# Attention loops: joining a group's chunk maxima one VectorE instruction later, and multiplying by the reciprocal of the denominators on GpSimd

## What is computed

```python
# L0_attn: full attention; L0_ffn: causal attention, then 8 experts; L2_ffn: 8 attention experts, top 2 of 8 per token
scores = einsum('bhqd,bhkd->bhqk', q, k) / sqrt(8)
p      = softmax(scores, axis=-1)      # exp(s - max) / sum
o      = einsum('bhqk,bhkd->bhqd', p, v)
out    = o.transpose(0, 2, 1, 3).reshape(B, S, D) @ Wo + bo
```

## Time and profile before

| | busy us | share of the span |
|---|---|---|
| TensorE matmul (PE) | 3294.3 | 81% |
| TensorE weight load (PEld) | 2143.1 | 53% |
| VectorE (DVE) | 3074.8 | 76% |
| ScalarE (ACT) | 2550.6 | 63% |
| GpSimd (POOL) | 429.8 | 11% |

### The profile page before, as it was taken

How to read it: one execution, slowest core, us unless ns; L and a number is a source line. 1 busy time by engine, 2 the same in 40 slices (tenths; PEclk the granted TensorE clock), 3 DMA queues, 4 the chain that set the end, 5 groups by cost and what they waited for, 6 DMA issues and landing times. The chain is left out here.

```text
span 4061.4 us, 129963 instructions
## 1 busy us (share of the span) xinstructions
PE 3294.3 (81%) x55226; PEld 2143.1 (53%) x55226; DVE 3074.8 (76%) x3739; ACT 2550.6 (63%) x4883; POOL 429.8 (11%) x1465
## 2 busy tenths in 40 slices
PE   2999999479997996555665639999999999999728
PEld 1566666235555673222444416666666666666415
DVE  4999999358893114998454449999999999999753
ACT  1799999337776344221211119999999999999622
POOL 0000000011000000000003001111111111111120
PEclk7899999779998997778876859999999999999858
DMA  5000000310000001330007874555455555554410
GB/s 113 9 7 9 7 9 5 88 25 11 9 7 2 24 18 47 145 116 29 6 5 117 242 195 120 124 123 125 121 128 128 120 130 120 129 127 117 108 33 11
DMA packets 208869, 305.77 MB, mean 75 GB/s; under 512 B 96508, under 2 KB 140994, under 8 KB 203150
## 3 DMA queue, kind: packets, MB, share of 16 engines
q1 hardware_dynamic: 203614, 292.37, 28.9%
q0 software_dynamic: 4688, 5.24, 0.6%
HBM read 228.17 MB, written 60.40 MB: 71 GB/s over the span
## 5 line engine op out<-in xcount | busy, mean ns | idle before, releaser
L843 ACT ACTIVATE channels_qk<-psum 128x512 f32<-128x512 f32 (+1 forms) x3906 | 2100.6, 594 | 286.2 <-PE psum L688 200.4
L905 DVE TENSOR_REDUCE l2f_chunk_max<-psum 128x2 f32<-128x1024 f32 x1176 | 1359.5, 1217 | 52.2 <-PE psum L663 48.4
L905 DVE TENSOR_REDUCE chunk_max<-psum 128x2 f32<-128x1024 f32 (+2 forms) x832 | 918.5, 1157 | 85.9 <-PE psum L663 46.1
L663 PE MATMUL psum<-l2f_k_parts,l2f_q_parts 48*128 48x512 bf16 x2352 | 715.0, 387 | 38.2 <-DVE l2f_chunk_max L905 26.8
L709 PE MATMUL psum<-channels_qk,l2f_v_and_ones 128*9 128x128 f32 x18432 | 718.2, 274 | 14.1 <-issue 14.1
L688 PE MATMUL psum<-l2f_q_parts,l2f_k_parts 51*128 51x128 bf16 x9224 | 727.6, 217 | 2.0 <-ACT l2f_minus_max_rows L885 0.9
L663 PE MATMUL psum<-k_parts,q_parts 48*128 48x512 bf16 (+3 forms) x1664 | 425.1, 382 | 130.3 <-DMA q_parts<-q_rows_dram 93.2
L688 PEld LDWEIGHTS psum<-l2f_q_parts,l2f_k_parts 51*128 51x128 bf16 x9224 | 496.3, 94 | 41.9 <-ACT channels_qk L843 39.2
L709 PE MATMUL psum<-channels_qk,v_and_ones 128*9 128x128 f32 x12544 | 491.8, 275 | 1.8 <-ACT channels_qk L843 0.5
L709 PEld LDWEIGHTS psum<-channels_qk,l2f_v_and_ones 128*9 128x9 f32 x18432 | 396.7, 90 | 122.6 <-issue 16.5
L688 PE MATMUL psum<-q_parts,k_parts 51*128 51x128 bf16 x6272 | 430.6, 218 | 29.2 <-DMA q_parts<-minus_max_rows 10.6
(11 more groups left out here) (479 smaller groups left out, 3004.4 us busy)
## 6 DMA issues: line engine op xcount, KB each, us to landing
l2f_k_parts<-l2f_k_parts_dram SPq DMA_DIRECT2D x604, 192.0 KB, 3.6
l2f_v_and_ones<-expert_v_dram SPq DMA_DIRECT2D x148, 288.0 KB, 4.3
l1a_bc_rows<-ssm_rows_dram SPq DMA_DIRECT2D x16, 1024.0 KB, 5.5
expert_v_dram<-l2f_v_and_ones SPq DMA_DIRECT2D x8, 1152.0 KB, 4.4
channels_qk<-ssm_rows_dram SPq DMA_DIRECT2D x8, 1024.0 KB
expert_q_dram<-heads_out SPq DMA_DIRECT2D x8, 1024.0 KB
l2f_q_parts<-l2f_gathered_q_parts SPq DMA_DIRECT2D x456, 16.0 KB
k_parts<-k_rows_dram SPq DMA_DIRECT2D x4, 1536.0 KB
```

The source lines that it names most:

```text
L663: last = nc.tensor.matmul(c.ps[:, 2 * (n % 2) + j, 0:width], at.q[64 * j:64 * j + ROWS, tile % SLOTS, pair, :], kx(tile)[64 * j:64 * j + R ...
L843: nc.scalar.activation(at.prob[:, s % 4, j, 0:kts, :].rearrange("p k q -> p (k q)"), c.ps[:, ring.bank(i, n), 0:kts * 2 * P], ACT.Exp, sca ...
L905: v.tensor_reduce(at.mx[:, 4 * g + 2 * pp:4 * g + 2 * pp + 2, chunk], c.ps[:, 2 * (n % 2):2 * (n % 2) + 2, 0:span.width(tile, chunk)], X, ...
```

## The change

`finish_max` of a group is issued behind the first maximum of the next group of the same tile (three of four groups of a tile; the fourth stays at the end of the tile, as do those ahead of the loop). Its wait stays in the code. `divided` on VectorE becomes `inverted`, with the reciprocal alone, behind the fifth unit of the second group where it stood behind the fourth; it waits for `heads_ready` so that the denominators are not overwritten. The product is a GpSimd operation of the same shapes, ahead of the `split_max` of the second group (at the end of the tile in the causal loop). The closing wait for `heads_ready` moves from VectorE to GpSimd.

```diff
+            def divided(i):
+
+                pool.wait_ge(rden_ready, i)
+                dst = c.heads[:, 0:1, :] if routed else c.heads[:, i:i + 1, :]
+                g_.tensor_tensor(dst.rearrange("p a (h d) -> p (a h) d", d=HD), at.out[:, :, 0:HD],
+                                 at.rden[:, :].unsqueeze(2).to_broadcast([P, H, HD]), ALU.mult).then_inc(heads_ready, 1)
+
             def whole_tile(i):
                 if routed:
                     routed.load_index(pool, i + 2, i % 2)
                 for g in range(G):
                     group, tile = first_pass_of(i, g)
+                    if tri is None and g == 1 and i > 0:
+                        divided(i)
                     if routed and g == 0:
...
                     if exists(tile):
                         split_max(group, tile)
+                if tri is not None and i > 0:
+                    divided(i)
 
             done = each_tile(pool, whole_tile)
+            divided(done)
+            if not routed:
+                pool.wait_ge(heads_ready, tiles + 1)
...
-            def divided(i, n):
+            def inverted(i, n):
 
                 dve.wait_ge(s2_read, ring.read_when(i, n))
+                dve.wait_ge(heads_ready, i)
                 v.reciprocal(at.rden[:, :], at.out[:, :, HD]).then_inc(rden_ready, 1)
-                dve.wait_ge(rden_ready, i)
-                dst = c.heads[:, 0:1, :] if routed else c.heads[:, i:i + 1, :]
-                v.tensor_tensor(dst.rearrange("p a (h d) -> p (a h) d", d=HD), at.out[:, :, 0:HD],
-                                at.rden[:, :].unsqueeze(2).to_broadcast([P, H, HD]), ALU.mult).then_inc(heads_ready, 1)
 
             def whole_tile(i):
+                unfinished = None
                 for g in range(G):
                     group, tile = first_pass_of(i, g)
                     units = range(2 * span.chunks(tile)) if exists(tile) else []
-                    for unit in units[:4]:
+                    for unit in units:
                         maximum(group, unit, tile)
-                    if tri is None and g == 1 and i > 0:
-                        divided(i, ring.place(i, "out"))
-                    for unit in units[4:]:
-                        maximum(group, unit, tile)
-                    if exists(tile):
-                        finish_max(group, tile)
+                        if unit == 0 and unfinished:
+                            finish_max(*unfinished)
+                        if unit == 4 and tri is None and g == 1 and i > 0:
+                            inverted(i, ring.place(i, "out"))
+                    if not units and unfinished:
+                        finish_max(*unfinished)
+                    if not units and tri is None and g == 1 and i > 0:
+                        inverted(i, ring.place(i, "out"))
+                    unfinished = (group, tile) if exists(tile) else None
+                if unfinished:
+                    finish_max(*unfinished)
                 if tri is not None and i > 0:
-                    divided(i, ring.place(i, "out"))
+                    inverted(i, ring.place(i, "out"))
...
             done = each_tile(dve, whole_tile)
-            divided(done, ring.place(tiles, "out"))
-            if not routed:
-                dve.wait_ge(heads_ready, tiles + 1)
+            inverted(done, ring.place(tiles, "out"))
```

## The result

The changed kernel takes 4101.4 us (median of 5 runs, 4091.9 to 4103.6) against 4062.5: a ratio of 1.008, 95% interval 1.0066 to 1.0094. That is slower by 33 us by the ratio (27 to 38) and by 39 by the medians. The median lies outside the forecast range (4042 to 4092). The profiled execution, the fastest of the five, took 4091.9 us with a span of 4090.2, 28.8 us longer than before, and would just have lain inside.

A forecast was written before the change was run, and what follows sets the result against it. The prediction took neither VectorE nor TensorE alone to hold the loop. Routed loop +10.5, first loop -0.5, causal loop -4 and GpSimd's product +1 made +7 us on the median 4062.5: 4069.5, range 4042 to 4092.

The forecast's parts named there:

- What becomes late: Turnings of rows on TensorE: joining 1.01 us later against 0.62 slack, 0.45 wait at three of four turnings, 0.19 left over.
- What bounds the kernel: Full loops: neither engine holds the loop alone; TensorE can gain 0.28 us a routed tile, 0.8 a first-loop tile.
- The joining and the product on VectorE: VectorE, routed tile: later joining saves 0.37 us, the product's leaving 0.33, together 0.70.
- rival D: Joining saves nothing on VectorE, rows 0.12 us later still, +0.15 a tile, some 4076; chance 0.06.
- rival C: GpSimd's product takes 1.3 us, late for `turn_heads`: 0.5 us a routed tile, about 4088; chance 0.07.
- the handoff from GpSimd to TensorE: Before a turning of rows: some 0.06 us added, from a ScalarE row; GpSimd's may be up to 0.1.
- slack of 0.62: Between the end of GpSimd's four operations and TensorE's turning of the rows: 0.62 us to spare in the kernel before.
- cushion of 0.26: Behind a turning, TensorE's wait for ScalarE in the second pass absorbs a delay of up to about 0.26 us.
- Group 2: Routed tile, second group: VectorE starts its last unit as today, so its turning adds again +0.16 us.
- The first loop: Late turnings and TensorE's 0.8 us of excess a tile cancel: -0.03 a tile, -0.5 us, bounds -13 and +8.
- The causal loop: Rows are turned whole groups after joining, so only VectorE's saving acts: -4 us (0 to -10).
- B: No cushion behind the turnings: each late one costs its full 0.45 us, about 4093; chance 0.14.

The follow-up runs named there:

- e3: Changed kernel with the rows of full tiles turned one step later: ratio 1.0051 to the kernel before, first-loop tile 37.82 us.
- e5: Changed kernel, rows turned one step later (first loop all, routed loop steps 10 and 18), routed third group joined in its old place: 0.9968 of the kernel before.
- e7: Kernel before with the first operation of GpSimd's split made three times more in three of four groups (0.83 us delay): one run, 4096.8 us.
- e8: Kernel before with the first operation of GpSimd's split made four times more in three of four groups (1.11 us delay): ratio 1.0131.
- e10: Changed kernel with the later joining kept only for the first group in the two full loops: one run, 4078.4 us.
- e11: Changed kernel with the later joining kept only for the third group in the two full loops: one run, 4074.6 us.
- e2: Changed kernel with the joining back in its old place, so only the product moved to GpSimd: ratio 0.9991 to the kernel before.
- e9: Changed kernel measured again, unaltered: ratio 1.0083 to the kernel before.
- e1: Kernel before with the later joining alone, the product still on VectorE: ratio 1.0069 to the kernel before.
- e6: Kernel before with the first operation of GpSimd's split made two times more in three of four groups (0.55 us delay): one run, 4082.1 us.
- e4: Kernel before with the rows of full tiles turned one step later: ratio 1.0092 to the kernel before.

## Why the prediction was wrong

The mechanism was right and two of its sizes were wrong: how late a turning becomes, and how much of that TensorE regains before the next. Both stand under "What becomes late". The three loops were forecast to grow by 6 us (10.5-0.5-4) and grew by 26.9 in the trace. That is 21 us of the 32 between the forecast (4069.5) and the median; 10 more are the distance from the profiled execution to the median, which stays open.

*What bounds the kernel.* Right: TensorE's own tile is only 0.1 to 0.3 us shorter than VectorE's in the routed loop, and some 0.8 in the first loop, and a lighter VectorE gains only that. With the turnings out of the way the first loop gave 0.75 us a tile (e3, e5), against 0.8 read from the rows. The routed loop gave 0.15 (e5) of 0.28.

*The joining and the product on VectorE.* Right. The joining follows at 1.13 us instead of 1.25, so the rival D is not borne out: an instruction that waits for its predecessor's end starts 0.12 us later than one that doesn't. The Trainium skill ("VectorE: DVE Perf Modes", section "The DRAIN you can't avoid") says that a semaphore between chained operations costs nothing extra, measured on a row of copies; the reductions here don't bear that out. The same section says that a next operation that is not held back starts earlier, and with that the rows agree (1.13 between starts, under the 1.22 that one takes). GpSimd's product took 0.41 us against the 0.43 of the nearest row and was hidden: rival C didn't occur. Its only wait was behind the last tile.

*What becomes late.* The mechanism was right: three turnings a tile wait for GpSimd, and 0.24 us of each wait vanishes behind them (0.26 predicted; the rows above, e7 and e8). Two sizes in this term were wrong, and they make the miss in the loops.

First, the handoff from GpSimd to TensorE. I took 0.06 from the nearest row, one from ScalarE, and it is 0.12; and the turning itself holds the weighted values 0.03 longer (2839.04 to 2839.07; in the kernel before both start at 2750.90). With that TensorE is 0.28 us late at unit 12, where I had 0.19. Beside a slack of 0.62 and a cushion of 0.26 these are small, but what is left after both is a small difference, and it grew by half, three times a tile.

Second, "Group 2: VectorE starts this group's last unit when it does today". It doesn't. Behind the first late turning VectorE waits for TensorE (0.23 at unit 11 in the rows above), so it starts the second group's last unit 0.1 later than before, and the second turning comes at +0.39 and not at +0.16. The third comes at +0.68 and not at +0.3. I had let TensorE regain 0.1 ahead of the second turning and only the third group inherit lateness; instead each late turning hands on what it costs. e7 to e8 and e10 show it: past the cushion each turning costs its full excess, about 0.28 us. So the routed tile is +0.68 instead of +0.3, 36 tiles +24.5 instead of +10.5 (36 x 0.3 is 10.8; the slip changes nothing); the loop measured +23.6.

*The first loop*, -0.03 a tile predicted, +0.28 measured. The same step failed: I had VectorE 0.2 us ahead at the last turning, but it starves behind each late turning and is not ahead. TensorE's spare time did not help either: where it arrives early at a turning it waits longer (0.79 us at step 18, 0.63 at step 10), since the turning's time is set by the joining. Here spare time ahead of a wait bought nothing; only spare time behind it would have.

*The causal loop*, -4 predicted, -1.4 in the trace, within the bounds given. The sign isn't safe: with the lighter VectorE this loop took 406.6 to 406.8 us in five traces (after, e3, e5, e10, e11) and 410.1 and 410.3 in two (e2, e9), against 407.9 to 408.1 in the traces with VectorE's old work. What divides the two was not tried.

*The rivals and the range.* B's 4093 is nearer to the measured 4101 than the forecast and close to the profiled 4092, but by luck: its mechanism, no cushion, is refuted by e7 and e8. I had bounded the routed loop at +0.7 a tile, which is nearly what it came to, yet put the range's upper end below what both bounds together give (4063+25+8 = 4096, with the causal gain left out). A bound that is reached by two terms of 0.05 to 0.1 us in a difference of 0.2 is no remote end.

*What stays open.* The median lies 10 us above the profiled execution. The trace of e9, 12.9 us longer than the other of the same kernel, has the same tiles (39.53 and 38.85). About 11 us of the difference has arisen before the routed loop begins: 2.6 ahead of the first loop, 3.8 between it and the causal loop, 3.6 in the causal loop, 1.0 behind it. The mean granted clock was 0.894 in place of 0.899. What sets that off was not tried. Why e2's whole gains less than its tiles is open in part. Its routed tiles are longer than their shortest at one place, the step from unit 5 to unit 6: 1.23 us in the median and 1.10 in the kernel before, 6.6 us more over the loop. The same place stands out in e1, e5, e6, e7 and e8 (4.8 to 7.6 us) and not in before, after, e9, e10 and e11 (0.3 to 0.7 us). All six ran on chips on which the kernel before takes 17 to 20 us longer than on the others, and no single edit is common to them, so it may belong to the chip; no trace of the kernel before on such a chip was kept (e3 and e4, on such a chip too, don't show it, but they lose more in the steps just ahead).

## What to carry to other kernels

Before delaying the head of a chain to fill a bubble, measure the slack at the chain's far end, on the in-order engine that waits for it, and count every handoff: here 0.12 us was gained three times a tile on VectorE, and 1.01 us of delay was put into a slack of 0.62. Move the consumer along with the producer, and then look at what is issued behind the consumer. In this loop, where two engines pace each other, a stall on one was handed to the other and came back at the next such place, so the prices of repeated stalls added; what is regained must be shown, not assumed.

## What the runs showed of the hardware

A VectorE instruction that waits for its predecessor's end starts 0.03 us after it (the joining, 1.25 after the start of a maximum of 1.22), one that doesn't starts 0.09 us before it (chunk maxima of 1.22 us every 1.13). Handoffs differ by engine: 0.12 us from GpSimd's end to TensorE's first load, 0.08 to 0.09 from VectorE's end to GpSimd's start (2837.81 to 2837.90), 0.06 from ScalarE to TensorE. A product of 128x128 took GpSimd 0.41 us and VectorE 0.29, 1.4 times.
